# Two loads per head group whose rows are taken in another order: the outermost dimension of the source becomes 24 where it was 3

## The reference, cut to what matters

```python
q = _rope((x @ Wq.T).reshape(B, S, H, hd).transpose(0, 2, 1, 3))   # H = 16 heads of hd = 8
k = _rope((x @ Wk.T).reshape(B, S, H, hd).transpose(0, 2, 1, 3))
scores = jnp.einsum('bhqd,bhkd->bhqk', q, k) * scale
attn = jax.nn.softmax(jnp.where(causal, scores, min), axis=-1)
out = jnp.einsum('bhqk,bhkd->bhqd', attn, v)
```

## Time and profile before

| | us |
|---|---|
| Median of 3 runs (655.25, 657.92, 1727.74) | 657.92 |
| The profiled execution | 656.71 |
| Its span | 655.0 |
| PE busy in it | 564.1 (86%) |
| DVE busy | 401.0 (61%) |
| ACT busy | 310.4 (47%) |
| POOL busy | 212.5 (32%) |

### The profile page before, as it was taken

One profiled execution on the slowest core, in us unless ns is written; L12 is line 12 of the kernel. 1 busy time (PEld: TensorE's weight loads), 2 busy tenths in 40 slices (PEclk: granted clock), 3 DMA queues, 4 the chain that ended last, 5 costly groups with the idle time before them and its releaser, 6 DMA issues.

```text
span 655.0 us, 10075 instructions
## 1 busy us (share of the span) xinstructions
PE 564.1 (86%) x3634; PEld 311.1 (48%) x3634; DVE 401.0 (61%) x932; ACT 310.4 (47%) x589; POOL 212.5 (32%) x276
## 2 busy tenths in 40 slices
PE   3884998888887898999978999999999998899873
PEld 1732444444343454544435555545576446644642
DVE  6374877685684565675765675756646765534453
ACT  2311765666453664466434655554445432563221
POOL 4562444153442632660353211414322110220101
PEclk9685999999888899999998999999999999999987
DMA  9322113111334433211571122225314120000000
GB/s 269 103 88 102 39 46 111 59 53 41 122 111 77 114 88 128 110 67 61 103 182 46 56 51 42 47 77 116 92 21 86 30 51 1 19 2 1 0 18 16
DMA packets 26657, 46.55 MB, mean 71 GB/s; under 512 B 3216, under 2 KB 12336, under 8 KB 26032
## 3 DMA queue, kind: packets, MB, share of 16 engines
q1 hardware_dynamic: 26608, 45.91, 25.8%
HBM read 27.62 MB, written 17.83 MB: 69 GB/s over the span
## 4 chain that ended last, share of the span: by engine, by line
PE 60%; DVE 15%; SPq 6%; DMA 5%; ACT 5%; issue 4%; POOL 3%; DVEq 0%; POOLq 0%; ACTq 0%
PE ps L564 13%; PE ps L627 11%; PE ps L521 9%; PE ps L492 6%; DVE NM L1123 4%; PE ps L515 4%; PE ps L494 3%; PE ps L489 3%; PE ps L748 2%; DVE stats L1107 2%; PE ps L677 2%; SPq L441 2%; PE ps L571 2%; DMA KS<-scr_k 2%; PE ps L610 1%
## 5 line engine op out<-in xcount | busy, mean ns | idle before, releaser
L1123 DVE TENSOR_REDUCE NM<-ps 128x1 f32<-128x512 f32 (+3 forms) x352 | 219.3, 638 | 119.2 <-PE ps L494 111.5
L785 ACT ACTIVATE PG<-ps 128x512 f32<-128x512 f32 x320 | 181.5, 596 | 169.3 <-PE ps L521 86.8
L521 PE MATMUL ps<-QS,K 128*128 128x512 f32 x320 | 117.9, 453 | 0.0
L494 PE MATMUL ps<-maskb,identb 128*128 128x128 bf16 x512 | 108.8, 231 | 0.0
L564 PE MATMUL ps<-PG,V 128*32 128x512 f32 (+3 forms) x1024 | 97.9, 456 | 8.8 <-POOL PG L1070 6.2
L492 PE MATMUL ps<-K,QS 96*128 96x256 f32 (+3 forms) x256 | 83.6, 371 | 10.4 <-DVE NM L1123 10.2
L489 PE MATMUL ps<-KS,QS 96*128 96x256 bf16 (+3 forms) x256 | 72.3, 317 | 16.7 <-DVE NM L1123 15.6
L515 PE MATMUL ps<-QS,KS 128*128 128x128 bf16 (+3 forms) x256 | 64.1, 313 | 12.2 <-DMA QS<-MP 6.7
L1029 POOL TENSOR_TENSOR whole<-terms 128x512 f32<-128x512 f32 x28 | 35.5, 1269 | 109.4 <-DVEq L1216 107.8
L521 PEld LDWEIGHTS ps<-QS,K 128*128 128x128 f32 x320 | 50.9, 191 | 39.1 <-issue 19.6
L494 PEld LDWEIGHTS ps<-maskb,identb 128*128 128x128 bf16 x512 | 51.4, 100 | 38.0 <-issue 30.5
(11 more groups left out here) (153 smaller groups left out, 670.5 us busy)
## 6 DMA issues: line engine op xcount, KB each, us to landing
scr<-QC SPq DMA_DIRECT2D x24, 512.0 KB, 3.1
QS<-scr SPq DMA_DIRECT2D x32, 256.0 KB
QS<-scr_q SPq DMA_DIRECT2D x16, 288.0 KB
KS<-scr_k SPq DMA_DIRECT2D x16, 288.0 KB
QS<-scr SPq DMA_DIRECT2D x64, 64.0 KB
scr_k<-room SPq DMA_DIRECT2D x20, 128.0 KB, 1.9
scr_q<-room SPq DMA_DIRECT2D x12, 128.0 KB, 1.9
x<-in_x SPq DMA_DIRECT2D x4, 256.0 KB, 6.2
```

Of the source, the lines that this page charges most:

```text
L494: return pe.matmul(dst[:, P * (k - 1):P * k], identb[:], maskb[:, 0, :], start=False, stop=True)
L521: mm = pe.matmul(bank.rearrange("p (h q) -> p h q", h=HG), keys[:, SEQ[n] % 2, P * j:P * j + P], QS2[:, heads, P * i:P * i + P], start=(ke ...
L785: act.activation(PG[:, n % 2, unit_place(LAYER[n], (u + k) % UNITS), :], ps[:, ST0 + (u + k) % 3, :], ACT.Exp, scale=scale).then_inc(exp_d ...
L1123: dve.tensor_reduce(dst, src, AX.X, ALU.max, negate=True).then_inc(fill_read, 1)
```

## The change

The two transfers of `load1` fill the same rows 0 to 71 with the same data in another order. Before, the source was walked as repetition (3), then part and dim (24), then 2048 contiguous elements (4 heads x 512, 4 KB). Now it is walked as part and dim (24), then repetition (3), then the same 2048 elements. Row 3 (8 a + d) + r of `QS1` and `KS1` holds what row 24 r + 8 a + d held, in both alike, so the sum over the rows is over the same pairs. Count and size of the transfers, their place in SP's stream, the destination's 72 rows, and all semaphores are as before. No instruction of another engine changes.

```diff
                 heads = slice(HG * g, HG * g + HG)
-                q_parts = scr_q[b].rearrange("a (d h) t -> (a d) h t", h=H)[:, heads, :]
-                k_parts = scr_k[b, 0:3].rearrange("a (d h) t -> (a d) h t", h=H)[:, heads, :]
-
-                sp.dma_start(QS1[0:72, heads, :], bass.AP(q_parts.tensor, q_parts.offset, [[0, 3], *q_parts.ap]))\
-                  .then_inc(stack1_in[g], 16)
-                sp.dma_start(KS1[0:72, heads, :], bass.AP(k_parts.tensor, k_parts.offset, [[P * T, 3], *k_parts.ap]))\
-                  .then_inc(stack1_in[g], 16)
+                rows = [[H * T, 24], [0, 3], [1, HG * T]]
+                sp.dma_start(QS1[0:72, heads, :], bass.AP(scr_q, (3 * b * P + HG * g) * T, rows)).then_inc(stack1_in[g], 16)
+                rows = [[H * T, 24], [P * T, 3], [1, HG * T]]
+                sp.dma_start(KS1[0:72, heads, :], bass.AP(scr_k, (5 * b * P + HG * g) * T, rows)).then_inc(stack1_in[g], 16)
```

## The result

| | us |
|---|---|
| Median of 5 runs of the changed kernel (650.08 to 653.42) | 651.86 |
| Median of 5 runs of the kernel before (655.25 to 657.92, and one of 1727.74) | 656.26 |
| Ratio, with its 95% interval | 0.991 [0.9886, 0.9934] |
| The profiled execution of the changed kernel; its span | 650.08; 648.4 |

The kernel is 0.9% faster, within the 2% band. The forecast was 649.1 from a profiled execution of 656.71, a ratio of 0.988, just outside the interval on the fast side. The profiled execution of the changed kernel is the fastest of its five.

What follows compares the result with a forecast made beforehand. PE, busy 86% of the span, was taken to bound the kernel, so only its waits for transfers count. 656.7 - 6.7 (stall at 56 us) - 0.9 (stall at 119 us) = 649.1 us; 8-in-10 range 643.5 to 654.

Steps and rivals of the forecast that it cites:

- Where PE stands still for a transfer: PE's list shows three waits that end with a transfer: 6.7, 4.1 and 0.9 us, each once.
- the first stall: PE's wait near 56 us for the maxima's small transfer goes altogether, gain 6.7 us; 4.1 with the slowest landing.
- The count of engines: Each stack load goes over 12 engines instead of 3; bounds 3 and 16.
- The rate of the loads: Sequence 0's eight loads drain at 328 GB/s instead of 82, in 7.2 us instead of 28.8.
- Both delays have one origin: Late issue (56.59) and slow landing (6.53 us) of the maxima's transfer both come from loads draining one per 3.5 us.
- The landing of 1.9 us: The maxima's transfer, issued at 52.6, lands 1.9 us later, at 54.5; bounds 1.84 and 6.53 us.
- PE comes at 56.5: PE's arrival at the first stall is held fixed, because it follows DVE's reductions there and not a load.
- The stall at 119 us: PE's wait for a load of sequence 1 goes, gain 0.9 us; bounds 0 and 0.94.
- The clock: After resuming at 56.5 PE's clock takes the same course as before, term 0; bounds 1.5 us gain or loss.
- The other loads and the jam near 250 us: Remaining loads of sequences 1 to 3, and layer 2's jammed query stores: each worth 0; the stores' bounds 0 and 3.2.
- More comes back: Rival: unjammed stretches near 250 us give 3.2 us and the clock 1.5 as well, 644.4; chance 0.12.
- Slower: issuing costs more: Rival: SP's issue time per load grows with the engines fed, past 3.3 us; end at 669 to 674; chance 0.03.

Runs made afterwards that it cites:

- e1_seq0: New order for sequence 0's four groups' loads only, sequences 1 to 3 as in the kernel before: 651.49 us, ratio to before 0.9896.
- e3_thirds: Kernel before, rows in the old order, each load cut into three transfers of 24 rows: 652.49 us, ratio to before 0.9912.
- e5_spaced: Kernel before, with only group 3's load of sequence 0 moved behind the maxima's transfer of group 0: 650.32 us, ratio to before 0.9882.
- e4_act: Kernel before, with three of sequence 0's eight loads issued on ACT's queue instead of by SP: 658.71 us, ratio to before 0.9984.
- e2_rest: New order for the loads of sequences 1 to 3 only, sequence 0 as in the kernel before: 658.63 us, ratio to before 1.0019.
- the second (657.75 to 652.08): The changed kernel run once more, unaltered, beside the kernel before on the same chip: 652.08 us, ratio to before 0.9912.

## Why the prediction was right, point by point

- **Where PE stands still for a transfer, and that the first stall goes: right.** 6.7 was forecast. The profile shows 5.8, and 6.6 with the first load's start set equal; e1_seq0 alone has the whole gain.
- **The count of engines: right.** 12 small packets a load, and a DMA share of 0.73. The rule of the Trainium skill (DMA: Bandwidth & Descriptors, Why a DMA increments its semaphore by 16 and not by 1) is borne out at a new value: outermost sizes of 24 and 72 gave 12, and of 24 and 24 in e3_thirds also 12.
- **The rate of the loads: too high.** 328 GB/s were forecast by scaling, 214 measured. It changes no term: the loads are through by 41.2 us, and the maxima's transfer comes at 54. The loads before were also slower through than the prediction has it (27 to 56): their last packets pass at 59.7.
- **"Both delays have one origin": right; what I took from it for e4_act, wrong.** The jam of the loads on 3 engines makes both the late issue (4.1 us behind ACT's copy) and the slow landing (6.53), and e5_spaced shows that with the backlog both go. But the prediction's weight lay on SP ("nothing stands before them on SP any more"), and read so it gave e4_act a gain of 5 to 7 us; there was none, because a freed SP leaves the landing to take 10.34 us. The number isn't luck: the change takes away the backlog itself.
- **The landing of 1.9 us: right.** Issued at 53.73, its last packets pass at about 55.4, 1.7 us later and two before PE comes.
- **"PE comes at 56.5": a little late,** 57.48, of which 0.86 is the later start that the clock brought. 0.1 remains.
- **The stall at 119 us, 0.9: removed, but not found in the time.** The wait is gone in the profiles of the change and of e2_rest. e2_rest is not faster for it (1.0019), and e1_seq0, which keeps 0.5 of it, is as fast as the change. The term was over-sized; less than 1 us is also less than what executions of one program differ by.
- **The clock, 0: small, on the side of a loss.** PE worked at 1.2 GHz from 63.26 to 66.5 before (0.50 up to 66, 0.73 from 66 to 67), and from 57.48 to 61.8 after (0.50 up to 61, 0.59 from 61 to 62): 4.3 us instead of 3.3, some 0.5 us of work lost. The clock ahead of the stall, at 11.9 to 18 us, cost the 0.86 of the later start; the prediction had no term for it, and between executions it goes either way (e1_seq0's first load is issued at 26.30).
- **The other loads and the jam near 250 us, 0: right,** by e2_rest.
- **The rivals.** "More comes back" needed something at 250 us, and there is nothing. "Slower: issuing costs more" didn't come: 0.76 us an issue for 0.69.

Taken together the medians moved by 4.4 us in the first comparison and 5.7 in the second (657.75 to 652.08), where 7.6 was forecast. The term of 0.9 that isn't there and the 0.5 of the clock bring 7.6 to about 6.2. The rest is within the intervals and no run here splits it further.

## What to carry to other kernels

Look at the DMA share while one kind of transfer runs alone: about 0.2 points at 3 engines of 16, and the completions counted among the small packets say it exactly. Then ask not how fast that transfer is but who shares its engines: a 12 KB transfer on PE's path waited behind the last load, for group 3, and the stores of the next sequence, 0.54 MB that nobody needed so soon. Putting the bulk on more engines, or issuing the part that is needed last after the urgent one, gave 4 to 7 us; issuing part of the bulk from another engine's queue gave nothing. And a jam that every view shows, as at 250 us here, is worth nothing as long as the engine that sets the end is not behind it.

## What the runs showed of the hardware that I had not expected

- Two queues share an engine packet by packet. In e4_act 4 KB packets of ACT's queue and 1 KB packets of SP's took turns one for one, at 66 GB/s together, and the 12 KB behind SP's stores landed after 10.34 us instead of 1.7. Moving the loads to another queue didn't free the engines.
- Twelve engines are not four times three. Three carried 82 GB/s, 27 each; twelve carried 214, 18 each, and in e3_thirds 164, 14 each. A 4 KB packet took 159 ns (median, 36.4 to 43.2 us) over three engines, and 229 and 314 ns in the two kernels with twelve (31 to 37 us).
- SP takes loads of 24 large packets an engine without being held until the fifth; the sixth is held for 5.4 us in each of the kernels that issue six or more in the old order on SP (before, e2_rest, e5_spaced). With 6 large packets an engine none of eight is held.
